# Counting edges per block: sums of two one-hot columns instead of four, and more matmuls to add them

## The chip, the cores and the metric

The kernel runs on one core of a Trainium2 chip. A core has five engines that run their own instruction streams: TensorE (PE in the profile, its weight loads PEld), VectorE (DVE), ScalarE (ACT), GpSimd (POOL) and SyncE (SP, which here only issues DMAs). They wait for one another by semaphores. The metric is the device time of one execution in microseconds (us); lower is better. Times are compared as medians of several runs.

## The reference

A graph with 3125 nodes (256 features each) and 103125 edges `src`, `dst`, `edge_weight1`. Cut to what matters:

```
h   = layernorm(x)
msg = silu(concat(h[src], h[dst], edge_weight) @ mW1 + mb1)
msg = silu(layer_norm(msg) @ mW2 + mb2)
agg = segment_sum(msg, src, 3125)
x   = x + h + silu(concat(h, agg) @ uW1 + ub1) @ uW2 + ub2
# then a feed-forward layer for the 1561 nodes with the highest router score
```

`setup_inputs` sorts the edges by `dst`, so `src`, by which messages are summed, comes in no order. The kernel has to sort the edges by the block of `src` first.

## The kernel before

The 3125 nodes are cut into 25 blocks of 125. The program has these stages, one after the other: counting and placing (up to about 160 us), routing of edge records into sorted order (to about 410 us), the edge stage with the two message layers (to about 1800 us) and the node stage. The change touches the first alone.

**What counting computes.** Each of 128 partitions holds 806 edges. They are handled in 62 supersteps of 13 columns (`COLS`), two supersteps to a *group*, so there are 31 groups (`i` in the code). For every edge the stage finds its place among the edges of the same block: how many edges of that block stand before it. In a group:

- `equal(i)` (VectorE, L700) writes the one-hot tile `eq`: for each of the 2 x 13 columns of edges, 25 numbers that are 1 where the edge's block is b. That is 650 elements in a partition. `eq` is a ring of four groups (`EQR`), and `equal` is called three groups ahead.
- `sums(i)` (GpSimd, L490 and L495) adds neighbouring columns: `two[t] = eq[t] + eq[t-1]`, then `four[t] = two[t] + two[t-2]`, with zero columns in front. `two` is one buffer, `four` a ring of two.
- `totals(i)` (TensorE, L578) adds up whole supersteps: four matmuls with a matrix of ones over columns 0, 4, 8 and 12 of `four`, 50 elements wide (both supersteps at once).
- ScalarE (L343) copies this total out of PSUM into `tot`. Between two such copies it has other work: casts of the edge data and the sums and squares of layernorm (`tallies`).
- `count(i)` (TensorE, L587 and L589) makes, in a PSUM bank for each superstep, the number of equal blocks before each edge. One matmul with a strictly triangular matrix counts within a column (325 wide), and matmuls with ones add the earlier columns of the superstep: with sums of four columns these are shifted by 1, 5 and 9 columns and 300, 200 and 100 elements wide.
- `starts(i)` (VectorE, L708, L710, L712) makes from `tot` where each block begins, and `bases(i)` (TensorE, L597, two matmuls 325 wide) adds it to the same banks.
- `select(i)` (VectorE, L720 and L725) multiplies the banks with `eq` and reduces over the 25 blocks; that is the edge's place.

**The order of the work** is written out by hand. TensorE in step i: `totals(i+1)`, `count(i)`, `bases(i-1)`. VectorE in step i: `starts(i)`, `select(i-1)`, `equal(i+3)`. GpSimd: `sums(i)` and behind it, in six of the groups, one piece of other work over all 806 columns (`plane`). Every engine runs its instructions in this order, so an instruction that waits holds up all behind it. GpSimd's `four(i)` waits until `count(i-2)` has read the ring's buffer (`s_cnt`), and `count(i)` waits for `select(i-3)` (`s_sel`), for three pairs of banks.

After the last `select` VectorE goes on by itself with the places of all edges, and routing follows.

Of the kernel before, what the change touches and what calls it, by code (L numbers as in the profile page):

```python
# [6 lines left out]
BF16 = mybir.dt.bfloat16  # L7
# [3 lines left out]
ALU = mybir.AluOpType  # L11
# [3 lines left out]
P = 128  # L15
# [3 lines left out]
BLOCKS = NODES // NB  # L19
COLS = 13  # L20
# [12 lines left out]
ROWS = TILES * P + P * WIN + P  # L33
DG = PAIRS // RING
EQR = 4
PCOLS = 3
PRING = 4
LAST = 18
# [12 lines left out]
def build(nc, io):  # L51
# [17 lines left out]
    with ExitStack() as whole:  # L69
        def alloc(stack, name, shape, dt):  # L70
            return stack.enter_context(nc.sbuf_tensor(name, shape, dt))

        def semaphore(stack, name):
            return stack.enter_context(nc.semaphore(name))
# [35 lines left out]
        with ExitStack() as ctx:  # L110
            def sb(name, shape, dt):
                return alloc(ctx, name, shape, dt)

            def sem(name):
                return semaphore(ctx, name)
# [12 lines left out]
            vals = sb("vals", [P, EC, PLANES], BF16)  # L128
            eq_words = EQR * 2 * (COLS + 1) * BLOCKS // 2
            eq = x_all[:, 6 * EC:6 * EC + eq_words].bitcast(BF16).rearrange("p (r h t b) -> p r h t b", r=EQR, h=2, b=BLOCKS)  # L130
            two = sb("two", [P, 2, COLS + 2, BLOCKS], BF16)
            four = sb("four", [P, 2, 2, COLS, BLOCKS], BF16)
            prod = sb("prod_e", [P, 2 * COLS, BLOCKS], F32)
            place = x_all[:, 2 * EC:3 * EC]
            r_all = x_all[:, 3 * EC:4 * EC]
# [19 lines left out]
            tb_i = sb("tb_i", [P, PG], I32)  # L155
            or_ = sb("or_", [P, 2, COLS - PCOLS, P], BF16)
            orp = [half[:, k * PCOLS * P // 2:(k + 1) * PCOLS * P // 2].bitcast(BF16).rearrange("p (t r) -> p t r", t=PCOLS)
                   for half in (f1, f2) for k in range(PRING // 2)]
# [3 lines left out]
            onesb = sb("onesb", [P, P], BF16)  # L162
# [60 lines left out]
            s_f1 = sem("s_f1")  # L223
            s_eq = sem("s_eq")
            s_sums = sem("s_sums")
            s_four = sem("s_four")
            s_base = sem("s_base")
            s_cnt = sem("s_cnt")
            s_fresh = sem("s_fresh")
# [189 lines left out]
            def _(pool):  # L419
# [1 line left out]
                pool.memset(dst_i[:, TAIL:EC], 0).then_inc(s_pads, 1)  # L421
                pool.memset(ew_f[:, TAIL:EC], 0.0).then_inc(s_pads, 1)
                pool.memset(eq[:, :, :, 0:1, :], 0.0).then_inc(s_sums, 1)
                pool.memset(two[:, :, 0:2, :], 0.0).then_inc(s_sums, 1)
                pool.memset(mb1_z[:, :], 0.0).then_inc(s_mb1, 1)
                pool.memset(onesb[:, :], 1.0).then_inc(s_pool, 1)
                pool.iota(iota_n[:, :], pattern=[[1, P]], base=0, channel_multiplier=0,
# [55 lines left out]

                def sums(i):
                    pool.wait_ge(s_eq, i + 1)
                    if i:
                        pool.wait_ge(s_four, i)
                    else:
                        pool.wait_ge(s_sums, 2)
                    pool.tensor_tensor(two[:, :, 2:COLS + 2, :], eq[:, i % EQR, :, 1:COLS + 1, :],  # L490
                                       eq[:, i % EQR, :, 0:COLS, :], ALU.add).then_inc(s_sums, 1)
                    pool.wait_ge(s_sums, i + 3)
                    if i >= 2:
                        pool.wait_ge(s_cnt, i - 1)
                    pool.tensor_tensor(four[:, i % 2, :, :, :], two[:, :, 2:COLS + 2, :], two[:, :, 0:COLS, :],  # L495
                                       ALU.add).then_inc(s_four, 1)

                def last_row():
                    pool.wait_ge(s_last, 16)
                    pool.wait_ge(s_to_all, 1)  # L500
                    pool.wait_ge(s_pool, 19)
                    pool.wait_ge(s_four, 4)
                    pool.tensor_copy(w_parts[WP:P, 0, :], w_last[WP:P, :]).then_inc(s_parts, 1)
                    pool.wait_ge(s_parts, 1)
                    pool.tensor_tensor(w_parts[WP:P, 1, :], w_last[WP:P, :], w_parts[WP:P, 0, :],
                                       ALU.subtract).then_inc(s_parts, 1)
                    pool.wait_ge(s_parts, 2)

                for i in range(SUPERS // 2):
                    sums(i)  # L510
                    if i == 3:
                        last_row()
                    plane(i)
                    if i == 16:
                        pool.wait_ge(s_tally, BLOCKS)
                        pool.tensor_scalar(neg_mean[:, :], tally[:, 0, :], -1.0 / D, None, ALU.mult).then_inc(s_mean, 1)
# [10 lines left out]
                def pool_columns(s):  # L527
                    if s >= PRING:
                        pool.wait_ge(s_win, s - PRING + 1)
                    for k in range(PCOLS):  # L530
                        c = s * COLS + COLS - PCOLS + k
                        ins = pool.tensor_scalar(orp[s % PRING][:, k, :], iota_n[:, :], r_all[:, c:c + 1], None,
# [34 lines left out]
            def _(pe):  # L567
                pe.wait_ge(s_pool, 3)

                def bank(s):  # L570
                    return psK[:, 2 * (s // 2 % 3) + s % 2, 0:COLS * BLOCKS].rearrange("p (t b) -> p t b", b=BLOCKS)

                def totals(i):
                    pe.wait_ge(s_four, i + 1)
                    if i:
                        pe.wait_ge(s_tot, i)
                    for t in range(0, COLS, 4):
                        mm = pe.matmul(psX[:, 0:2 * BLOCKS].rearrange("p (h b) -> p h b", h=2), onesb[:, :],  # L578
                                       four[:, i % 2, :, t, :], start=(t == 0), stop=(t == COLS - 1))
                    mm.then_inc(s_totp, 1)  # L580

                def count(i):
                    if i >= 3:
                        pe.wait_ge(s_sel, i - 2)
                    for h in range(2):
                        to = bank(2 * i + h)
                        pe.matmul(to[:, :, :], tri[:, :], eq[:, i % EQR, h, 1:COLS + 1, :], start=True, stop=False)  # L587
                        for d in range(1, COLS, 4):
                            mm = pe.matmul(to[:, d:COLS, :], onesb[:, :], four[:, i % 2, h, 0:COLS - d, :],  # L589
                                           start=False, stop=False)  # L590
                    mm.then_inc(s_cnt, 1)

                def bases(i):
# [6 lines left out]
                    mm.then_inc(s_rank, 1)  # L600

                totals(0)
                for i in range(SUPERS // 2 + 1):
                    if i < SUPERS // 2:
                        if i + 1 < SUPERS // 2:
                            totals(i + 1)
                        count(i)
                    if i:
                        bases(i - 1)
# [4 lines left out]
                for k in range(2):  # L614
                    mm = pe.matmul(psC[0:1, 0:D], bcol[:, k:k + 1], w2raw[:, k, :], start=(k == 0), stop=(k == 1))
# [24 lines left out]
                def route(s):  # L640
# [4 lines left out]
                    for t in range(COLS):  # L645
                        marks = or_[:, s % 2, t, :] if t < COLS - PCOLS else orp[s % PRING][:, t - COLS + PCOLS, :]
                        mm = pe.matmul(psK[:, s % 3, 0:PLANES * WIN], marks,
# [18 lines left out]
                for g in range(TG):  # L666
# [4 lines left out]
                    for k, plane in enumerate((0, 4, 5)):  # L671
                        mm = pe.transpose(psR[:, g % 2, k, 0:n], recT[0:n, g, :, plane], identb[0:n, 0:n])
# [3 lines left out]
            def _(dve):  # L676
# [21 lines left out]
                def equal(i):  # L698
                    c = 2 * COLS
                    V.tensor_tensor(eq[:, i % EQR, :, 1:COLS + 1, :],  # L700
                                    blk[:, i * c:(i + 1) * c].rearrange("p (h t) -> p h t", h=2).unsqueeze(3).broadcast_to(
# [67 lines left out]
                def windows(s):  # L769
                    if s >= 2:  # L770
                        dve.wait_ge(s_win, s - 1)
                    own = slice(s * COLS, (s + 1) * COLS)
                    mine = slice(s * COLS, (s + 1) * COLS - PCOLS)
                    V.tensor_tensor(or_[:, s % 2, :, :],
# [785 lines left out]
```

## Time and profile before

| | us |
|---|---|
| median of 3 runs | 2132.21 (2132.2 to 2133.16) |
| the profiled execution | 2126.56 |
| its span, first to last instruction | 2124.8 |
| counting: first `equal` to the end of the last `select` | 15.8 to 154.0 |
| PE busy, whole span | 1848.7 (87%) |
| DVE busy, whole span | 1847.5 (87%) |
| POOL busy, whole span | 1483.0 (70%) |

A row of the timeline has the start in us from the span's start, the length in us, the engine, the line, the operation, what it writes and reads, and the shape; `x3` means three instructions merged; in brackets stands how long the engine was idle before it and what ended that. A group's row has the number of instructions, the busy time, the mean of one in ns, and the idle time before them. Matmuls overlap: a matmul's own length (from its start until its result has left the array) is longer than the distance to the start of the next one. Matmul rows with `x2` or more span from the first start to the last end.

### The profile page before, as it was taken

To read this page: it belongs to the slowest core of one execution; us is meant where nothing else is said; L and a number is where in the kernel's file an instruction comes from. 1 tells how busy PE (TensorE), PEld (TensorE's weight loads), DVE (VectorE), ACT (ScalarE), POOL (GpSimd) and SP (SyncE) were. 2 spreads that over 40 slices of the span, in tenths; PEclk is the share of its full clock that TensorE was granted. 3 is DMA by queue.
4 is the path that set the end of the run, shared out by engine and by line. 5 is a ranking of instruction groups with operands and counts; after the bars stand their busy time and mean duration, and the time that the engine had idled before them with its cause. 6 is when DMAs were issued, how large, how long until landed. Compare 5 with 4: busy or idle time off the path is not lost. (4 is left out here: it accounts for less than half of the span.)

```text
span 2124.8 us, 46537 instructions
## 1 busy us (share of the span) xinstructions
PE 1848.7 (87%) x11277; PEld 1603.5 (75%) x11278; DVE 1847.5 (87%) x4642; ACT 1501.9 (71%) x3084; POOL 1483.0 (70%) x1393
## 2 busy tenths in 40 slices
PE   3554665259999999999999999999999999799996
PEld 1333554258999999999999989999999899577775
DVE  5788999568999999999999999999999999655895
ACT  2322332149999999999999999999999999323322
POOL 8767888487888888888888888888888886503000
PEclk9996887579999999999999999999999999899998
DMA  4000000245333333333333333433333335101001
GB/s 133 1 0 12 30 30 25 90 121 160 104 104 101 107 100 107 103 103 104 104 104 101 106 101 107 102 105 104 104 104 101 106 102 65 43 1 21 10 1 61
DMA packets 109820, 169.16 MB, mean 80 GB/s; under 512 B 42785, under 2 KB 79571, under 8 KB 109517
## 3 DMA queue, kind: packets, MB, share of 16 engines
q0 software_dynamic: 43168, 114.55, 21.1%
q1 hardware_dynamic: 61086, 48.90, 7.5%
q10 hardware_dynamic: 5516, 5.08, 0.8%
q8 instruction: 26, 0.43, 0.1%
q14 instruction: 24, 0.20, 0.0%
HBM read 156.30 MB, written 11.74 MB: 79 GB/s over the span
## 5 line engine op out<-in xcount | busy, mean ns | idle before, releaser
L961 POOL DMA_INDIRECT g_rows<-b_table,idx_ring x816 | 849.4, 1041 | 237.2 <-issue 212.3
L1097 PE MATMUL ps<-w2g,nT 128*128 128x256 f32 x3432 | 815.4, 381 | 1.2 <-ACT rec L997 1.2
L1097 PEld LDWEIGHTS ps<-w2g,nT 128*128 128x128 f32 x3432 | 620.8, 191 | 68.6 <-ACT rec L997 1.4
L1004 ACT ACTIVATE normed<-act,rec 128x255 f32<-128x255 f32 x858 | 467.6, 596 | 88.0 <-DVE rec L1162 83.5
L1069 PE MATMUL psH<-a_sb,ohT 128*128 x1716 | 345.3, 324 | 43.2 <-DVE ohT L1176 39.4
L1069 PEld LDWEIGHTS psH<-a_sb,ohT 128*128 128x128 f32 x1716 | 257.9, 192 | 97.7 <-issue 74.9
L1196 DVE BATCH_NORM_STATS2 rec<-act 128x6 f32<-128x256 f32 x858 | 316.6, 409 | 1.9 <-ACT act L1018 1.9
L1202 DVE TENSOR_TENSOR low<-rec,high 128x512 fp32r<-128x512 f32 x429 | 301.5, 703 | 1.1 <-ACT high L1010 1.1
L1190 DVE TENSOR_TENSOR g_rows<-psH,g_rows 128x512 f32<-128x512 f32 x429 | 292.5, 682 | 10.0 <-DMA g_rows<-b_table,rec 8.3
L1018 ACT ACTIVATE act<-g_rows 128x512 f32<-128x512 f32 x429 | 267.5, 624 | 19.7 <-DVE g_rows L1190 19.5
L1010 ACT ACTIVATE high<-rec 128x512 fp32r<-128x512 f32 x429 | 266.7, 622 | 0.2
L997 ACT ACTIVATE rec<-ps 128x512 f32<-128x512 f32 x429 | 251.3, 586 | 11.8 <-PE psG L1080 11.8
L1089 PE MATMUL psM<-identf,normed 128*128 128x128 f32 x1716 | 258.7, 273 | 0.5 <-ACT nT L1014 0.5
L1014 ACT ACTIVATE nT<-psM 128x512 f32<-128x512 f32 x429 | 249.4, 581 | 3.9 <-PE ps L1097 3.9
L950 POOL TENSOR_TENSOR rec<-rec,exph 128x6 f32<-128x6 f32 x143 | 224.2, 1568 | 15.2 <-DVE rec L1154 12.2
L1079 PE MATMUL psG<-high,ohf 128*125 128x256 f32 x858 | 223.3, 283 | 11.7 <-DVE agg L1129 11.7
L1080 PE MATMUL psG<-low,ohf 128*125 128x256 f32 x858 | 223.5, 282 | 0.0
L1089 PEld LDWEIGHTS psM<-identf,normed 128*128 128x128 f32 x1716 | 201.0, 141 | 0.7 <-issue 0.7
L1181 DVE TENSOR_TENSOR ohf<-rec 128x250 fp32r<-128x250 f32 x429 | 185.9, 433 | 0.0
L1129 DVE TENSOR_TENSOR agg<-psG,agg 125x256 f32 x429 | 176.3, 411 | 0.6 <-PE psG L1080 0.4
L1079 PEld LDWEIGHTS psG<-high,ohf 128*125 128x125 f32 x858 | 159.4, 186 | 14.8 <-DVE low L1202 14.4
L1176 DVE TENSOR_SCALAR ohT<-loc_rows,node_col 125x256 fp32r<-125x256 bf16 x429 | 163.1, 380 | 4.3 <-DMA loc_rows<-loc_d 4.3
(206 smaller groups left out, 2397.3 us busy)
## 6 DMA issues: line engine op xcount, KB each, us to landing
loc_rows<-loc_d SPq DMA_DIRECT2D x143, 187.5 KB
g_rows<-b_table,idx_ring POOLq DMA_INDIRECT x816
h_sb<-in_x SPq DMA_DIRECT2D x1, 3125.0 KB
b_table<-b_out SPq DMA_DIRECT2D x25, 125.0 KB
x_all<-in_x ACTq DMA_DIRECT2D x1, 3125.0 KB
out<-x_all SPq DMA_DIRECT2D x5, 625.0 KB
ohT<-ew_d SPq DMA_DIRECT2D x143, 9.0 KB
idx_ring<-rec SPq DMA_DIRECT2D x136, 3.0 KB
```

Of the source, the lines that this page charges most:

```text
L961: pool.indirect_dma_start(g_rows[:, j, n, :], None, b_table[:, :], bass.IndirectOffsetOnAxis(ap=which, axis=0)).then_inc(s_gather[j], 16)
L997: nc.scalar.activation(msg[:, (j - 15) % 3, :, :], ps2[:, (j - 15) % 2, :, :], ACT.Silu).then_inc(s_msg, 1)
L1004: ins = nc.scalar.activation(normed[:, (j - 10) % 2, n, 0:D - 1], act1[:, (j - 10) % RING, n, 0:D - 1], ACT.Identity, scale=rstd_e[:, g % ...
L1010: nc.scalar.activation(high[:, (j - 15) % 3, :, :], msg[:, (j - 15) % 3, :, :], ACT.Copy).then_inc(s_high, 1)
L1018: nc.scalar.activation(act1[:, (j - 4) % RING, :, :], g_rows[:, (j - 4) % RING, :, :], ACT.Silu).then_inc(s_act1, 1)
L1069: mm = pe.matmul(psH[:, j % 2, n, :], ohT[:, k, n, :], rows, start=(part == 0), stop=(part == 1))
L1079: pe.matmul(to, ohf[:, k, n, :], high[:, k, n, :], start=(n == 0), stop=False)
L1089: mm = pe.transpose(psM[:, (j - 11) % 2, n, q, :], normed[:, (j - 11) % 2, n, q * P:(q + 1) * P], identf[:, :])
L1097: mm = pe.matmul(ps2[:, (j - 13) % 2, n, :], nT[:, (j - 13) % 2, n, q, :], w2g[:, q, :], start=(q == 0), stop=(q == 1))
L1190: V.tensor_tensor(g_rows[:, k, :, :], psH[:, j % 2, :, :], g_rows[:, k, :, :], ALU.add).then_inc(s_hid, 1)
L1196: ins = V.bn_stats(stat[:, q // 3, 2 * (q % 3) + n, :, :].rearrange("p h w -> p (h w)"), act1[:, q, n, :])
L1202: V.tensor_tensor(low[:, k, :, :], msg[:, k, :, :], high[:, k, :, :], ALU.subtract).then_inc(s_low, 1)
```

## The change

GpSimd no longer makes `four`. `sums(i)` is one instruction, which writes `two` in a ring of three groups, without the zero columns in front. `count` therefore needs matmuls with ones at shifts 1, 3, 5, 7, 9 and 11 (300, 250, 200, 150, 100 and 50 wide) for each superstep, and `totals` seven matmuls, over columns 0, 2, ..., 12. The wait of GpSimd for TensorE is now for `count(i-3)`.

```diff
+TWOS = 3
-            two = sb("two", [P, 2, COLS + 2, BLOCKS], BF16)
-            four = sb("four", [P, 2, 2, COLS, BLOCKS], BF16)
+            two = sb("two", [P, TWOS, 2, COLS, BLOCKS], BF16)
...
-                pool.memset(two[:, :, 0:2, :], 0.0).then_inc(s_sums, 1)
...
                 def sums(i):
                     pool.wait_ge(s_eq, i + 1)
-                    if i:
-                        pool.wait_ge(s_four, i)
-                    else:
-                        pool.wait_ge(s_sums, 2)
-                    pool.tensor_tensor(two[:, :, 2:COLS + 2, :], eq[:, i % EQR, :, 1:COLS + 1, :],
-                                       eq[:, i % EQR, :, 0:COLS, :], ALU.add).then_inc(s_sums, 1)
-                    pool.wait_ge(s_sums, i + 3)
-                    if i >= 2:
-                        pool.wait_ge(s_cnt, i - 1)
-                    pool.tensor_tensor(four[:, i % 2, :, :, :], two[:, :, 2:COLS + 2, :], two[:, :, 0:COLS, :],
-                                       ALU.add).then_inc(s_four, 1)
+                    if i == 0:
+                        pool.wait_ge(s_sums, 1)
+                    if i >= TWOS:
+                        pool.wait_ge(s_cnt, i - TWOS + 1)
+                    pool.tensor_tensor(two[:, i % TWOS, :, :, :], eq[:, i % EQR, :, 1:COLS + 1, :],
+                                       eq[:, i % EQR, :, 0:COLS, :], ALU.add).then_inc(s_two, 1)
...
-                    pool.wait_ge(s_four, 4)
+                    pool.wait_ge(s_two, 4)
...
                 def totals(i):
-                    pe.wait_ge(s_four, i + 1)
+                    pe.wait_ge(s_two, i + 1)
...
-                    for t in range(0, COLS, 4):
+                    for t in range(0, COLS, 2):
                         mm = pe.matmul(psX[:, 0:2 * BLOCKS].rearrange("p (h b) -> p h b", h=2), onesb[:, :],
-                                       four[:, i % 2, :, t, :], start=(t == 0), stop=(t == COLS - 1))
+                                       two[:, i % TWOS, :, t, :], start=(t == 0), stop=(t == COLS - 1))
...
-                        for d in range(1, COLS, 4):
-                            mm = pe.matmul(to[:, d:COLS, :], onesb[:, :], four[:, i % 2, h, 0:COLS - d, :],
+                        for d in range(1, COLS, 2):
+                            mm = pe.matmul(to[:, d:COLS, :], onesb[:, :], two[:, i % TWOS, h, 0:COLS - d, :],
                                            start=False, stop=False)
```

TensorE's order in one step of counting, before: the second superstep's `count` (325, 300, 200 and 100 wide; `tri` is the triangular matrix, `onesb` the ones, `x_all` holds `eq`), then `bases`, then the next `totals`.

```order
L587 MATMUL psK<-x_all,tri 128x325
L589 MATMUL psK<-four,onesb 128x300
L589 MATMUL psK<-four,onesb 128x200
L589 MATMUL psK<-four,onesb 128x100
L597 MATMUL psK<-we,onesb 128x325 x2
L578 MATMUL psX<-four,onesb 128x50 x4
```

The same place on TensorE with the change:

```order
L581 MATMUL psK<-x_all,tri 128x325
L583 MATMUL psK<-two,onesb 128x300
L583 MATMUL psK<-two,onesb 128x250
L583 MATMUL psK<-two,onesb 128x200
L583 MATMUL psK<-two,onesb 128x150
L583 MATMUL psK<-two,onesb 128x100
L583 MATMUL psK<-two,onesb 128x50
L591 MATMUL psK<-we,onesb 128x325 x2
L572 MATMUL psX<-two,onesb 128x50 x7
```

The order of the calls is the same; each superstep's `count` has three matmuls more and each `totals` three more.

GpSimd's order around group 4, before (`a_sb` is written by the `plane` pieces):

```order
L467 TENSOR_TENSOR a_sb<-a_sb,vals 128x806
L490 TENSOR_TENSOR two<-x_all 128x2x325
L495 TENSOR_TENSOR four<-two 128x650
L490 TENSOR_TENSOR two<-x_all 128x2x325
L495 TENSOR_TENSOR four<-two 128x650
L470 TENSOR_SCALAR a_sb<-a_sb 128x806
```

The same place and a little further on with the change:

```order
L466 TENSOR_TENSOR a_sb<-a_sb,vals 128x806
L489 TENSOR_TENSOR two<-x_all 128x650 x2
L469 TENSOR_SCALAR a_sb<-a_sb 128x806
L489 TENSOR_TENSOR two<-x_all 128x650 x2
L472 TENSOR_SCALAR a_sb<-a_sb 128x806
```

Each group has one instruction on GpSimd where it had two; the pieces of other work keep their places. VectorE's and ScalarE's orders are unchanged.

## Rows read from the trace of the kernel before

**Rows 1.** The page: TensorE's granted clock in 40 slices, in tenths.

```profile
PEclk9996887579999999999999999999999999899998
```

**Rows 2.** Waits in 40 to 150 us: total us, times, longest.

```profile
DVE prod_e L720 <- PE psK L597: 24.8, 19, 2.1
```

**Rows 3.** Timeline, 109.4 to 118.4 us: one circle over two groups.

```profile
109.45 0.83 DVE L700 TENSOR_TENSOR x_all<-x_all,psV 128x650 bf16<-128x650 f32 x1
...
110.36 1.42 POOL L490 TENSOR_TENSOR two<-x_all 128x650 bf16<-128x650 bf16 x1 [0.61 <-DVE x_all L700]
...
111.87 1.30 POOL L495 TENSOR_TENSOR four<-two 128x650 bf16<-128x650 bf16 x1
...
113.22 0.35 PE L578 MATMUL psX<-four,onesb 128*128 128x50 bf16 x4 [0.96 <-POOL four L495]
...
113.39 0.45 PE L587 MATMUL psK<-x_all,tri 128*128 128x325 bf16 x1
...
114.10 0.83 DVE L700 TENSOR_TENSOR x_all<-x_all,psV 128x650 bf16<-128x650 f32 x1
...
114.85 0.24 DVE L708 SCALAR_TENSOR_TENSOR sm<-agg,psV 128x50 f32<-128x50 f32 x1
...
114.92 0.74 PE L597 MATMUL psK<-we,onesb 128*128 128x325 bf16 x2
...
115.78 0.83 DVE L720 TENSOR_TENSOR prod_e<-psK,x_all 128x650 f32<-128x650 f32 x1
...
116.64 0.83 DVE L725 TENSOR_REDUCE x_all<-prod_e 128x26 f32<-128x650 f32 x1
117.51 0.83 DVE L700 TENSOR_TENSOR x_all<-x_all,psV 128x650 bf16<-128x650 f32 x1
```

**Rows 4.** Timeline, 145 to 154 us: the last groups.

```profile
149.22 0.75 PE L597 MATMUL psK<-we,onesb 128*128 128x325 bf16 x2
149.71 0.24 DVE L708 SCALAR_TENSOR_TENSOR sm<-agg,psV 128x50 f32<-128x50 f32 x1
...
150.53 0.83 DVE L720 TENSOR_TENSOR prod_e<-psK,x_all 128x650 f32<-128x650 f32 x1
...
150.56 0.61 PE L597 MATMUL psK<-we,onesb 128*128 128x325 bf16 x2 [0.58 <-DVE we L712]
...
153.14 0.83 DVE L725 TENSOR_REDUCE x_all<-prod_e 128x26 f32<-128x650 f32 x1
```

**Rows 5.** PE alone in four stretches: length, busy (instructions), granted clock, DMA.

```profile
109.80:117.80 8.00, 4.89 (x28) 1.00 0.00 0
145.40:150.90 5.50, 4.89 (x26) 1.00 0.00 0
...
229.40:232.80 3.40, 0.80 (x15) 1.00 0.16 47
178.20:181.60 3.40, 1.69 (x19) 1.00 0.00 2
```

**Rows 6.** Timeline, 36 to 40 us: the wait for the node rows.

```profile
36.08 0.42 ACT L338 ACTIVATE b_out<-h_sb 125x256 f32<-125x256 f32 x1 [8.50 <-DMA h_sb<-in_x]
...
37.28 0.32 PE L578 MATMUL psX<-four,onesb 128*128 128x50 bf16 x4 [5.55 <-ACT agg L343]
...
39.81 0.83 DVE L720 TENSOR_TENSOR prod_e<-psK,x_all 128x650 f32<-128x650 f32 x1 [1.85 <-PE psK L597]
```

**Rows 7.** Groups of GpSimd in 15 to 154 us.

```profile
L521 POOL TENSOR_TENSOR rstd<-rstd,exph 125x25 f32<-125x25 f32 x1 | 4.4, 4362 | 0.1
L482 POOL TENSOR_TENSOR vals<-a_sb 128x806 bf16<-128x806 f32 x1 | 2.9, 2898 | 0.0
L470 POOL TENSOR_SCALAR a_sb<-a_sb 128x806 f32<-128x806 f32 x1 | 2.3, 2282 | 0.0
```

**Rows 8.** Groups in 109.8 to 117.8 us: weight loads of `count` and of `totals`.

```profile
L589 PEld LDWEIGHTS psK<-four,onesb 128*128 128x128 bf16 x12 | 1.7, 145 | 0.9
...
L578 PEld LDWEIGHTS psX<-four,onesb 128*128 128x128 bf16 x8 | 0.4, 115 | 4.4 <-POOL four L495 4.4
```

More of the change, by code:

```diff
@@ L225, in build @@
             s_sums = sem("s_sums")
-            s_four = sem("s_four")
+            s_two = sem("s_two")
             s_base = sem("s_base")
```

## The prediction

> **What bounds the kernel now.** I read the page first, for the clock and the stages, then the timeline of counting, since the change touches nothing else, and last the waits there. In counting no engine is busy throughout. The waits name a circle: VectorE waits for the matmuls of `bases`, 24.8 us in all [rows 2], GpSimd waits for VectorE's `equal` (0.61 us, rows 3), and TensorE waits for GpSimd's `four` [rows 3]. The timeline gives its length [rows 3]. From an `equal` at 109.45: 0.91 us to the start of `two`, 1.51 from there to `four`, 1.35 to `totals`, 0.17 to `count`, 1.53 to `bases`, 0.86 to `select` and 1.73 to the `equal` two groups on, at 117.51. That is 8.06 us for two groups (two such circles run interleaved), or 4.03 a group. Over groups 2 to 27 the mean is somewhat longer, 4.19 us: the pieces of other work on GpSimd, 2.3 to 2.9 us each [rows 7], delay the circle now and then.
>
> The start is held by something else. ScalarE waits 8.50 us for the DMA of the node rows, and with it TensorE for the copy of a total, until 37.28 [rows 6]. What the change gains before that is lost there; only from 37.28 on does it count.
>
> At the end VectorE's last `select` ends at 153.97 [rows 4] and the stages behind it start from there, so a shorter counting moves all that follows, one to one.
>
> **The clock in counting.** The page's clock digits show nearly full speed in the first slices [rows 1], and the windows 1.00 [rows 5], but the matmuls tell otherwise. Of two matmuls of 325 columns at 149.22, the whole takes 0.75 us; at 150.56, after the engine had worked from 145.4 almost without a pause (4.89 of 5.50 us, rows 5), the same pair takes 0.61. The 0.14 saved is 325 columns at 1.2 GHz less 325 at 2.4 (0.27 − 0.135). And `count` before takes 1.53 us for 1850 columns, 0.83 ns a column, which is 1.2 GHz. So I take counting as running at 1.2 GHz up to 150 us. The Trainium skill ("TensorE: Matmul & The Clock Gate", Part 1) says that half rate is the default and that activity releases it, and gives start-to-start distances of N/1.2 and N/2.4 ns plus 2.5; by it the row's 1.00 can't be a granted full clock. The spacing here agrees with the skill, the window's figure doesn't.
>
> **The change part by part.**
>
> *GpSimd.* `four` goes: 1.35 us of the circle. `two` stays at 1.42, plus the 0.05 that `four` shows between its end and `totals` (1.35 − 1.30), so 1.47. Its output is now contiguous; I expect no difference, since `four` with the same 650 elements took 1.30, which bounds a gain at 0.12 us a circle. The removed memset lies before the first `equal` and costs nothing. The new ring wait is for `count(i-3)`. It never holds: `two(i)` waits for `equal(i)`, which stands behind `select(i-2)` and so behind `count(i-1)`. Queued behind it would be the pieces of other work, which nobody waits for closely.
>
> *TensorE.* `totals`: seven matmuls where four took 0.17, so 0.30. `count`: 2 x (325 + 300 + 250 + 200 + 150 + 100 + 50) = 2750 columns, at 1.2 GHz 2.29 us; at 2.4 GHz 1.15, and I take 1.20 for small gaps. `bases` is unchanged, 0.54 us of issue at 1.2 GHz and 0.27 at 2.4, by which its 0.86 to `select` falls to about 0.59.
>
> *The circle after, at 1.2 GHz:* 0.91 + 1.47 + 0.30 + 2.29 + 0.86 + 1.73 = 7.56, or 3.78 a group against 4.03. *At 2.4 GHz:* 0.91 + 1.47 + 0.30 + 1.20 + 0.59 + 1.73 = 6.20, or 3.10.
>
> *VectorE is late next.* Its own work of a group is 0.82 from L708 to L720 [rows 4], 0.86, 0.87, and 0.75 from `equal` to the next L708 [rows 3]: 3.30 us. So at 2.4 GHz not the circle but VectorE sets 3.30 a group. At 1.2 GHz the circle sets 3.78, and TensorE's own work is 0.30 + 2.29 + 0.54 = 3.13 a group.
>
> *Which clock?* Before, TensorE worked 4.89 us of 8.00 in counting and stayed at 1.2 GHz. With the change it works 3.13 of 3.78 a group, and from 37.28 on `totals`, `count`, `bases`, `totals`, `count`, `bases` follow without a pause for 6.2 us, since two groups of `two` are ready by then. The clock had risen by 150.56 after 4.89 of 5.50 us [rows 4, 5]. So I expect the rise in the 40s. Does it stay up? At 2.4 GHz TensorE works some 0.30 + 1.20 + 0.27 = 1.77 us of 3.30, and about 0.2 more with the tails. In 178.2 to 181.6 it worked 1.69 of 3.40 and the clock was at 1.00; before a fall (229.4 to 232.8) it had worked 0.80 of 3.40 [rows 5]. The new load lies nearer the first, so I take it to stay up.
>
> *The sum.* From `totals` at 37.28: `count` ends at 39.87, `select(2)` starts at 40.73, which is 0.92 later than before [rows 6], as `count` is longer and still slow. `select(3)` 3.30 later, 44.03. `equal(6)` at 42.46 leads by 0.91 + 1.47 + 0.30 + 2.29 + 0.86 to `select(4)` at 48.29. From there VectorE sets the pace: `select(5)` 51.6, `select(27)` 22 x 3.30 later, 124.2. The last three have no `equal`: 2.55, 2.55 and 1.73, and 1.73 for the last itself: 132.8, and 0.3 for the circle in the tail, 133.1. Against 153.97 that is 20.9. I take off 1 us for the 2.9 us piece on GpSimd (it makes `two` 1.1 us late; the circle has 0.4 to spare for two groups) and similar, and 1 us for a clock that rises a group later: 18.9, say 19. GpSimd's 4.36 us power for layernorm [rows 7] stays covered: it starts when the last `two` is done, some 2.4 us after the last `equal`, ends at 7.1, and VectorE needs it 10.2 after that `equal`.
>
> The profiled execution at 2126.56 would become 2107.6. The median of the runs is 2132.21, 5.7 above that execution with the same program; I take 19 from it: **2113**.
>
> **The rivals.**
>
> 1. *The clock stays at 1.2 GHz in counting.* For: it did so in all steady groups before, and in rows the rise needs near-continuous work. Against: 3.13 of 3.78 us and the 6.2 us run. The same sum: `select(4)` at 48.3, 23 groups at 3.78 to `select(27)` at 135.2, then 3.7, 3.1, 1.73 and 1.73 for the tail: 145.5. Gain 8.5, less 0.5 for GpSimd: **2124**.
>
> 2. *The clock goes up and down.* At 2.4 GHz the engine pauses half of each group; if that lets it fall, the next groups run at 3.78, work is dense again, and it rises again. Routing shows such a change to and fro, at 0.80 us of work in 3.40 before a fall. Half the groups at each pace: 25 x 0.24 = 6 less than my sum, gain 13: **2119**. The Trainium skill (the same page, "A second HAM failure mode") describes matmul groups with small idles between them in which the clock oscillates; this is that rule, and no row of counting shows it yet, as the clock never rose there before 150.
>
> 3. *Slower: the weight loads of short matmuls show.* Each matmul has its own load, 145 ns in `count` and 115 in `totals` [rows 8]. If a matmul can't start sooner than 0.15 after the one before, `totals` takes 1.05 and `count` 2 x (0.27 + 0.25 + 0.21 + 4 x 0.15) = 2.66, together 3.71. The piece that they replace is 1.35 + 0.17 + 1.53 = 3.05, and from `two` 0.05 stays, so the change loses where both take over 3.00 us (it is 2.59 by columns). The circle becomes 8.7, 4.35 a group, 25 groups at +0.32 and the start: about +9, **2141**. Against it: the four 50-column matmuls of `totals` start within 0.17 us now, 42 ns apart, with 115 ns loads. The skill's page says, in Part 3, that weight loads overlap with running matmuls only for other row groups; by that this rival would be the forecast, but the 42 ns speak against it.
>
> 4. *Nothing to measure:* a gain under 4 us, where the rest gives it back: routing or the edge stage starting at a bad moment of TensorE's clock costs a few us at most. It needs rival 1 and this together: about **2130**.
>
> **How the numbers follow.** My case 0.62 (its own range 2110 to 2117, from 21 gained with nothing lost to 15 with a few slow groups), rival 2 0.16, rival 1 0.12, rival 4 0.06, rival 3 0.04. A difference under 0.2%, 4.3 us, can't be told from none here. Faster is then 0.90, same 0.06, slower 0.04. The range takes in my case, rivals 2 and 1: 2109 to 2126.
>
> **What would show it.** In the profile after: matmul pairs of `bases` of 0.75 us only up to the 40s, 0.61 or less behind that; `select` to `select` 3.30 us from about 50 on; VectorE's wait for `bases`, 24.8 us before, at a few us; `totals` in 0.47 us with seven matmuls; the last `select` ending at 134 to 135. Pairs of 0.75 throughout and 3.78 a group would be rival 1, a mixture rival 2, `totals` starts 0.1 or more apart rival 3. I am wrong altogether if counting ends before 140 and the whole is not shorter by as much.

## The result, and the profile after

| | before | after |
|---|---|---|
| median | 2132.2 us (4 runs) | 2108.86 us (4 runs, 2106.06 to 2111.7) |
| ratio | | 0.9896, 95% interval 0.9884 to 0.9908 |
| profiled execution, span | 2126.56, 2124.8 | 2107.55, 2105.8 |
| end of the last `select` | 154.0 | 132.5 |

23.3 us less, 1.1%; forecast were 19, to 2113. The measured median lies 0.14 us below the stated range, which began at 2109: the sign and the mechanism were right, and the size was somewhat too cautious.

The timeline after, one circle over two groups, answers to [rows 3]. The lines have moved: L694 is `equal`, L489 `two`, L572 `totals`, L581 and L583 `count`, L591 `bases`, L714 and L719 `select`, L702 the start of `starts`.

```profile
99.07 0.83 DVE L694 TENSOR_TENSOR x_all<-x_all,psV 128x650 bf16<-128x650 f32 x1
...
99.98 1.42 POOL L489 TENSOR_TENSOR two<-x_all 128x650 bf16<-128x650 bf16 x1 [1.88 <-DVE x_all L694]
...
101.46 0.35 PE L572 MATMUL psX<-two,onesb 128*128 128x50 bf16 x7 [1.46 <-POOL two L489]
...
101.65 0.30 PE L581 MATMUL psK<-x_all,tri 128*128 128x325 bf16 x1
...
102.85 0.45 PE L591 MATMUL psK<-we,onesb 128*128 128x325 bf16 x2
...
103.93 0.83 DVE L714 TENSOR_TENSOR prod_e<-psK,x_all 128x650 f32<-128x650 f32 x1
...
104.80 0.83 DVE L719 TENSOR_REDUCE x_all<-prod_e 128x26 f32<-128x650 f32 x1
...
105.67 0.83 DVE L694 TENSOR_TENSOR x_all<-x_all,psV 128x650 bf16<-128x650 f32 x1
```

Two groups take 6.60 us, 3.30 each, where they took 8.06. `count`, 2750 columns, lasts 1.20 us from L581 to L591: 0.44 ns a column, the 2.4 GHz rate; the pair of `bases` takes 0.45 us against 0.74 in [rows 3]. `select` starts 1.08 us after `bases` though some 0.6 would do, and its row has no idle time in brackets: VectorE was busy with what stands before it.

The waits in 40 to 133 us (total, times, longest) answer to [rows 2]:

```profile
POOL two L489 <- DVE x_all L694: 46.2, 21, 10.1
...
PE psX L572 <- POOL two L489: 36.8, 25, 2.1
DVE prod_e L714 <- PE psK L591: 3.2, 3, 2.7
```

VectorE's wait for `bases` fell from 24.8 us to 3.2, and 2.7 of that is the one after the DMA stall. The others now wait for VectorE.

TensorE in two stretches between changes of its clock (length, busy and instructions, granted clock, busy share of the DMA engines, GB/s), which answer to [rows 5]:

```profile
37.30:42.70 5.40, 4.96 (x39) 0.50 0.58 231
42.80:131.40 88.60, 48.72 (x601) 1.00 0.00 1
```

Behind the dense work right after the stall, 4.96 of 5.40 us, the clock rose at 42.8, and it stayed up to the end of counting, with TensorE busy 48.72 of 88.60 us. Here the matmul spacing and the granted clock agree. Before, the granted clock read 1.00 while the spacing was that of 1.2 GHz; that profile has no record of the clock before 150.9.

The start, which answers to [rows 6]:

```profile
37.63 0.25 DVE L702 SCALAR_TENSOR_TENSOR sm<-agg,psV 128x50 f32<-128x50 f32 x1 [7.70 <-ACT agg L343]
37.74 0.45 PE L572 MATMUL psX<-two,onesb 128*128 128x50 bf16 x7 [11.11 <-ACT agg L343]
...
41.16 0.83 DVE L714 TENSOR_TENSOR prod_e<-psK,x_all 128x650 f32<-128x650 f32 x1 [2.74 <-PE psK L591]
```

TensorE waits 11.11 us where it waited 5.55: the groups before were done sooner, and all of that went into the wait behind the DMA of the node rows.

### The profile page after: what moved, and what is told of

Its sections match the earlier page's. It is cut to its first block and busy times, and to the rows that moved or that the text cites. A ratio compares the mean times of both kernels' runs of the same rounds, so it can differ in the third digit from the quotient of the medians.

```text
span 2105.8 us, 47032 instructions
## 1 busy us (share of the span) xinstructions
PE 1828.9 (87%) x11556; PEld 1600.4 (76%) x11557; DVE 1849.6 (88%) x4642; ACT 1502.1 (71%) x3084; POOL 1443.2 (69%) x1361
```

## The experiments

Every kernel's profile gives the start of `select(27)`, the mean group from `select(4)` to it, and the time from the start of the last `select` to the end of the span, which the change doesn't touch:

| | select(27) | us a group | rest of the span | median |
|---|---|---|---|---|
| before | 144.5 | 4.17 | 1972.5 | 2132.2 |
| before again | 144.8 | 4.17 | 1980.2 | (2134.6, one run) |
| after | 123.7 | 3.30 | 1975.1 | 2108.9 |
| after again | 124.9 | 3.37 | 1974.3 | 2108.2 |
| before, TensorE filled | 138.2 | 3.89 | 1973.9 | 2123.9 |
| after, second addition kept | 147.6 | 4.30 | 1978.2 | 2134.8 |
| the same, TensorE filled | 145.3 | 4.23 | 1974.3 | 2129.5 |
| after, ring of two | 125.5 | 3.38 | 1975.7 | 2111.0 |
| after, roundings on ScalarE | 120.2 | 3.19 | 1976.4 | 2108.0 |
| the same, last piece moved | 117.6 | 3.08 | 1977.8 | 2104.3 |

The rows ran on different chips; runs of the kernel before beside them had medians of 2131.95 and 2130.18. Judge counting by the profiles and the whole by the ratios below, which are always to the kernel before on the same chip.

**Is the clock part of it? The kernel before, with TensorE filled.**

```diff
+FILL = 8
...
                     if i:
                         bases(i - 1)
+                    if i + 1 < SUPERS // 2:
+                        if i >= 2:
+                            pe.wait_ge(s_sel, i - 1)
+                        for _ in range(FILL):
+                            pe.matmul(psK[:, 2 * ((i + 1) % 3), 0:P], onesb[:, :], tri[:, :], start=True, stop=True)
```

> The kernel before, with four column sums, and eight extra matmuls of 128 columns in every group behind bases, in TensorE's pauses (their result is overwritten by the next count). Theory (part of the gain is TensorE's clock, which rises to 2.4 GHz when the engine works more of each group): bases pairs of 0.61 us instead of 0.75 from the first dense groups on, the circle 8.06 less 0.76 of count and 0.27 of bases, 7.03 us for two groups, 3.5 a group instead of 4.03 to 4.19; some 13 us less, about 2119. Rival (the clock is not what counts, GpSimd's shorter sums are all of it): 4.2 a group as before, 2132, or slower by what the extra matmuls delay.

Measured: 2123.92 us, ratio 0.9966 (0.9954 to 0.9979). More work, done sooner. The clock rose, but did not stay: 3.89 us a group on average. TensorE in three stretches with different clocks, and two matmuls of `bases` and the extra ones in the last undisturbed groups:

```profile
50.00:66.00 16.00, 6.95 (x84) 1.00 0.01 2
67.00:70.00 3.00, 2.89 (x22) 0.50 0.00 0
70.50:73.50 3.00, 1.15 (x15) 1.00 0.00 0
```

```profile
127.55 0.83 DVE L726 TENSOR_TENSOR prod_e<-psK,x_all 128x650 f32<-128x650 f32 x1
...
130.62 0.45 PE L598 MATMUL psK<-we,onesb 128*128 128x325 bf16 x2
130.92 0.61 PE L615 MATMUL psK<-tri,onesb 128*128 128x128 bf16 x8
...
134.52 0.83 DVE L726 TENSOR_TENSOR prod_e<-psK,x_all 128x650 f32<-128x650 f32 x1
```

From one `select` to the next but one, 127.55 to 134.52, are 6.97 us (7.03 expected), and so it is in eight circles in a row from 110 us on, where the clock stayed at 2.4 GHz. Where it fell in between, circles took 8.0 to 9.6; the longest of them also hold a piece of GpSimd's other work, as the 9.6 and 10.0 of the kernel before do. So the clock alone shortens the old circle by 1.1 us of 8.06.

**Does GpSimd's part count? The changed kernel with a second addition.**

```diff
                     pool.tensor_tensor(two[:, i % TWOS, :, :, :], eq[:, i % EQR, :, 1:COLS + 1, :],
-                                       eq[:, i % EQR, :, 0:COLS, :], ALU.add).then_inc(s_two, 1)
+                                       eq[:, i % EQR, :, 0:COLS, :], ALU.add).then_inc(s_add, 1)
+                    pool.wait_ge(s_add, i + 1)
+                    pool.tensor_tensor(spare[:, :, :, :], two[:, i % TWOS, :, :, :], two[:, i % TWOS, :, :, :],
+                                       ALU.add).then_inc(s_two, 1)
```

> The changed kernel, and GpSimd makes a second sum of the same size into a spare tile before it tells TensorE, so that GpSimd's part of the circle is as before (1.51 + 1.35 us) while TensorE's matmuls are the new ones. Theory with the clock up and staying up: circle 0.91 + 1.51 + 1.35 + 0.30 + 1.20 + 0.59 + 1.73 = 7.59, 3.80 a group against 3.30; about 12 us above the changed kernel, 2121, and still below the kernel before. With the clock low: 8.95, 4.48 a group, 2138, above the kernel before. A rival by which GpSimd is not on the path gives 2109.

Measured: 2134.75 us, ratio 1.0014 (1.0003 to 1.0026). The whole gain is gone, and a little more. GpSimd's addition took 1270 ns each, the circle 7.98 us with the clock mostly up and 8.9 to 9.1 otherwise, against 7.59 and 8.95 expected. The clock did not stay, so neither of the two expected times came, but one between, 4.30 us a group. It alternated like this:

```profile
57.50:64.10 6.60, 2.86 (x40) 1.00 0.01 2
64.30:71.00 6.70, 4.30 (x31) 0.50 0.00 0
71.20:77.80 6.60, 2.76 (x40) 1.00 0.00 0
78.00:88.00 10.00, 7.75 (x54) 0.50 0.01 2
```

TensorE was busy 2.86 and 2.76 of 6.60 us before the falls; in the changed kernel it was busy 48.72 of 88.60, and the clock held. The busy time does not decide alone: in the first experiment the clock held from 50 to 66 us with 6.95 busy of 16.00.

**Would more fill hold it up?** `FILL = 6` added to the kernel above, with the same edit as in the first experiment.

> The kernel with GpSimd's second addition kept and TensorE's new matmuls, and six extra matmuls of 128 columns a group in TensorE's pauses. Without them the clock went up and down and the mean group took 4.30 us, the two-group circle 7.98 at best and 8.9 while the clock was low. Theory (the falls of the clock cost the difference): with more work in each group the clock stays up, 3.99 us a group, the last groups 8 us sooner, about 2127, below the kernel before. Rival (the additions themselves on GpSimd make it slow): 4.3 us a group or more, 2135 or above.

Measured: 2129.54 us, ratio 1.0001 (0.9988 to 1.0013). The theory half failed: the clock still fell six times between 43 and 150 us. Most circles with the clock up took 7.41 us, less than the 7.98 that I had taken for the floor, and the mean group 4.23. Circles with a fall took up to 10.9 us against 7.41, though the longest also hold a piece of GpSimd's other work; that this much more work prevents the falls does not hold. A likely reason, not tested in this kernel, is that the extra matmuls don't fill a pause in which TensorE waits for GpSimd behind one of its long pieces.

**Is VectorE the bound? Two of its operations moved to ScalarE.**

```diff
+                    nc.scalar.activation(sm[:, 0, :, 1:BLOCKS + 1], psX[:, 0:2 * BLOCKS].rearrange("p (s b) -> p s b", s=2),
+                                         ACT.Copy, bias=WIN / 2 - 0.75).then_inc(s_st, 1)
                     nc.scalar.activation(tot[:, :, 2 * i:2 * i + 2].rearrange("p b s -> p s b"),
...
+                    nc.scalar.activation(sm[:, 0, :, 1:BLOCKS + 1], sm[:, 0, :, 1:BLOCKS + 1],
+                                         ACT.Copy, bias=MAGIC_W).then_inc(s_st, 1)
...
+                    nc.scalar.activation(sm[:, 1 + i % 2, :, 1:BLOCKS + 1], sm[:, 0, :, 1:BLOCKS + 1],
+                                         ACT.Copy, scale=1.0 / P, bias=-MAGIC_W / P).then_inc(s_st, 1)
...
-                    link(V.scalar_tensor_tensor(out=sm[:, 0, :, 1:BLOCKS + 1], in0=tot[:, :, 2 * i:2 * i + 2].rearrange("p b s -> p s b"),
-                                                scalar=WIN / 2 - 0.75, in1=magic_v.rearrange("p (s b) -> p s b", s=2), op0=ALU.add, op1=ALU.add))
-                    link(V.scalar_tensor_tensor(out=sm[:, 1, :, 1:BLOCKS + 1], in0=sm[:, 0, :, 1:BLOCKS + 1], scalar=-MAGIC_W,
-                                                in1=part_v.rearrange("p (s b) -> p s b", s=2), op0=ALU.add, op1=ALU.mult))
```

> The changed kernel with the two small VectorE operations of starts (0.51 us of VectorE a group) made on ScalarE, in three operations. Theory (VectorE's own work sets 3.30 us a group, the circle would allow 3.10): VectorE's work falls to 2.79, the circle sets 3.10; 25 groups at 0.20, about 5 us less, 2104. Rival (something else than VectorE sets 3.30): no difference. If ScalarE with three more operations a group comes too late: slower.

Measured: 2107.98 us, ratio 0.9896 (0.9876 to 0.9916). In counting the theory holds: most circles take 6.06 us, 3.03 a group, and VectorE waits for TensorE again (total, times, longest, 44 to 128 us):

```profile
DVE prod_e L725 <- PE psK L606: 11.4, 15, 2.7
```

So 3.30 was VectorE's own work, and the circle allows 3.03, not the 3.10 that was forecast. `select(27)` starts 3.5 us sooner, not 5: two circles took 8.7 and 8.2 us, when the clock fell at 86.5. In the median the 3.5 us do not show.

**What makes the clock fall there?** The last of GpSimd's long pieces, 2.9 us, runs just before. It was moved behind counting, first with the roundings on ScalarE, then alone in the changed kernel.

```diff
-                    plane(i)
+                    if i != 18:
+                        plane(i)
...
                 pool.tensor_tensor(rstd[:, :], rstd[:, :], exph[0:NB, :], ALU.pow).then_inc(s_rstd1, 1)
+                plane(18)
```

> The kernel with the roundings of starts on ScalarE, and the last piece of GpSimd's other work (2.9 us, group 18) moved behind the layernorm power, after counting. In the run before, this piece made TensorE's clock fall once and the two groups around it take 8.7 instead of 6.06 us. Theory: 3.03 us a group throughout, the last select 2.4 us sooner than there and some 6 us sooner than in the changed kernel; about 2103. Rival (the fall of the clock has another cause, or the piece then holds up routing): as before the move, about 2105 to 2108.

Measured: 2104.31 us, the median of three runs, ratio 0.9876 (0.9856 to 0.9895), the fastest version; these three, 2103.15 to 2104.41, lie below all four of the changed kernel on the same chip (2106.21 to 2109.99). A fourth run took 3836 us and is in neither figure. The clock stays up from 40.6 to 125.9 us, and all circles from group 14 up to the last groups take 6.06 or 6.07. Before group 14 some take up to 6.89, as they did without the move, so the mean is 3.08 a group and not 3.03.

> The changed kernel, unchanged, on the same chip as the others, to set the improved version beside it: 2109 within 3 us, 3.30 us a group.

Measured: 2108.18 us. This second profile of the changed kernel had a fall of the clock that the first had not. In its timeline GpSimd's piece is L481:

```profile
84.36 2.91 POOL L481 TENSOR_TENSOR vals<-a_sb 128x806 bf16<-128x806 f32 x1
...
86.99 1.42 POOL L489 TENSOR_TENSOR two<-x_all 128x650 bf16<-128x650 bf16 x1
...
88.46 0.47 PE L572 MATMUL psX<-two,onesb 128*128 128x50 bf16 x7 [2.16 <-POOL two L489]
...
89.00 1.09 PE L583 MATMUL psK<-two,onesb 128*128 128x300 bf16 x6
...
91.89 0.83 DVE L714 TENSOR_TENSOR prod_e<-psK,x_all 128x650 f32<-128x650 f32 x1 [1.70 <-PE psK L591]
```

`two` is late by 0.7 us, TensorE pauses 2.16 instead of 1.46, the clock falls at 88.3, six matmuls take 1.09 us and not 0.62, and VectorE waits 1.70: two interleaved circles of 8.25 for 6.59, by which all behind comes 1.66 us later. TensorE had been busy 1.84 us in the 4.2 before:

```profile
84.00:88.20 4.20, 1.84 (x23) 1.00 0.00 0
88.40:91.60 3.20, 3.14 (x24) 0.50 0.00 0
```

The first profile of the changed kernel has the same place 0.36 us later. There TensorE paused as long and had done as much, and the clock did not fall; the piece cost 0.15 us in each of the two circles:

```profile
88.80 0.35 PE L572 MATMUL psX<-two,onesb 128*128 128x50 bf16 x7 [2.14 <-POOL two L489]
```

```profile
84.36:88.56 4.20, 1.84 (x23) 1.00 0.00 0
```

So the pause and the work before it do not settle whether the clock falls. What does stays open.

> The changed kernel with only the last piece of GpSimd's other work (2.9 us, group 18) moved behind the layernorm power. Two of three profiles of the changed kernel (one of them with a ring of two) show one fall of TensorE's clock at 88 to 89 us, just behind this piece, and two circles of 8.2 us for 6.59. Theory (the piece makes the sum of group 19 late, TensorE pauses, and the clock may fall, by where in time the pause lies): no fall between 43 and 131 us, 3.30 us a group throughout, about 1 us below the changed kernel on average, 2107 to 2108. Rival (the falls come by chance wherever): a fall here too.

Measured: no fall; the clock stays at 2.4 GHz and all circles take 6.59 to 6.60 us up to the last groups.

```profile
42.30:130.80 88.50, 48.77 (x602) 1.00 0.01 1
```

Measured were 2251.64 us, but the times can't be set beside the others: on this chip the kernel before took 2262.68 us (ratio of this kernel 0.9949, 0.9923 to 0.9975). In the two profiles from this chip the edge stage is 134 and 141 us longer, and counting is not. The gain over the kernel before is 11.0 us here, half of the 22.0 on the chip of the repeat, though counting was as short; why is open, since the kernel before has no profile from this chip. Three profiles with the piece moved (two of them from this chip, with the next experiment's) show no fall there, against three of four with the piece in place that do. That speaks for the piece as what gives the occasion; the first profile of the changed kernel shows that the fall doesn't always come. Whether the move alone saves time in the whole was not shown, as the changed kernel was not run on this chip.

> The improved version once more, unchanged. One of its four executions took 3836 us, the three others 2103.2 to 2104.4. Theory (a disturbance of the chip that has nothing to do with the kernel): all near 2104, and about 4 us below the changed kernel. Rival (the edit has a rare slow case): another execution far above.

Measured: 2249.12 us on that slow chip, ratio 0.9942 (0.9922 to 0.9962), 12 runs from 2242.5 to 2255.3. No run far above came again; what made the one of 3836 us stays open. The 4 us below the changed kernel could not be tested here either; the runs overlap with those of the experiment before. Counting was as in the first run but for one other fall of the clock at 45 us, 3.07 us a group.

**Does the third buffer matter?** `TWOS = 2`.

> The changed kernel with a ring of two for the sums instead of three, so that GpSimd waits for count(i-2). Theory (that wait never ends last, since equal(i) stands behind count(i-1)): no difference, 2109. Rival (the third buffer carries part of the gain by letting GpSimd run ahead): slower by some us, groups above 3.30 us.

Measured: 2110.98 us, ratio 0.991 (0.9894 to 0.9927). I had said that the wait never ends last; with two buffers it does, eight times (44 to 133 us):

```profile
POOL two L489 <- DVE x_all L694: 22.2, 12, 1.9
POOL two L489 <- PE psK L583: 15.3, 8, 2.9
```

The reasoning was off by two groups: VectorE's order puts `equal(i)` behind `select(i-4)`, not `select(i-2)`, and so behind `count(i-3)` only. That covers the wait of a ring of three, for `count(i-3)`, and not that of a ring of two. The ring of two costs little: five circles of 6.71 to 6.87 us instead of 6.59, `select(27)` 0.6 us later than in the repeat of the changed kernel, which had a fall of the clock too. The 2.8 us between the medians are more than counting explains; the rest of the span was 1.4 us longer in this profile.

**How much does one profile say?**

> The kernel before, unchanged, for a second profile: the first profiled execution took 2126.56 us and the runs without a profile 2132.2. If profiled executions differ among themselves by the phase in which TensorE's clock changes come, this one may lie elsewhere between 2126 and 2133, with the difference in routing or the start of the edge stage; if a profile always takes less, it is near 2126.6 again.

Measured: 2134.56 us. Counting is the same to 0.3 us; after it, the rest took 1980.2 us and not 1972.5. Over all profiles on undisturbed chips this rest lies between 1972.5 and 1980.2, with no relation to the change (table). So the first profile of the kernel before had a short rest by chance. What sets the rest from run to run was not looked into.

## Why the prediction was right, point by point

- *The circle.* Right. Its terms hold: `two` to `totals` 1.48 (forecast 1.47), `count` 1.20 (1.20), `select` to `equal` 1.74 (1.73). One was too large: seven matmuls of `totals` before `count` take 0.19 us (101.46 to 101.65) and not 0.30. At 2.4 GHz they start 25 ns apart, except that the second starts 39 ns behind the first. `bases` to `select` was a little too large as well, 0.56 for 0.59 in the kernel with the roundings on ScalarE. That makes 6.06 of the 6.20, 3.03 a group and not 3.10.
- *The clock in counting before was 1.2 GHz.* Right, shown by the filled kernel: the same `bases` pair in 0.45 us, a circle 1.1 us shorter with more work in it. One reading behind it was wrong: the pair of 0.61 us at 150.56 lies across the rise of the clock at 150.9, and a pair wholly at 2.4 GHz takes 0.45, 0.30 less than at 1.2.
- *The clock rises after the stall and stays up.* Right for the first profile, from 42.8 to 131.5. In the repeat it fell once, which cost 1.66 us. The 1 us that I took off for a clock that rises a group later did not come. Rival 2, the clock up and down, came true in the variants with a longer circle, and in this kernel only as that one fall.
- *VectorE is late next, 3.30.* Right to the hundredth, and confirmed by taking work off VectorE.
- *What happens before the stall is lost.* Right: 11.11 us of wait for 5.55.
- *The ring wait never holds.* True from 40 to 133 us; before the stall it held once, for 1.6 us, which the stall took up. The step behind it was wrong: in steady groups `equal(i)` stands behind `count(i-3)`, not `count(i-1)` (the ring of two, above).
- *The start and the end.* `select(2)` at 41.16 (40.73), as `totals` began 0.46 later; `select(3)` 44.45 (44.03). From there it went better than I had it: `select(4)` at 47.75, not 48.29, because the clock had risen before `count(5)`. The last `select` started at 130.76 and ended at 132.5; my sum said 133.1, before I took off 2 us for the piece on GpSimd and a late clock. Of these 2 us, 0.15 came: the piece made `two` 0.7 us late and not 1.1.
- *The total.* 2107.6 for the profiled execution, measured 2107.55, is luck: counting gave 21.5 us, 2.6 more than my 18.9, and the rest took 2.6 more than in the first profile. The median, 2113 against 2108.86, shows the mis-sized terms: the 2 us taken off, and 0.6 of the sum. What is left of the 23.3, some 2 us, is in the spread of the rest.
- *Rival 3, weight loads of short matmuls.* It did not occur: 25 ns between matmuls whose loads take about 0.1 us each. The Trainium skill's sentence ("TensorE: Matmul & The Clock Gate", Part 3) that loads overlap only with matmuls on other rows of the array is not what these traces show, where loads on all 128 rows run beside the matmuls before them. Its Part 1 gives a floor of about 25 ns between starts, and there the trace agrees.
- *Rivals 1 and 4, the clock stays low, and nothing to measure:* did not occur. The give-back in the rest that rival 4 prices at a few us had no row behind it; the rest varied by 7.7 us over the profiles on undisturbed chips, with no relation to the change.

How the gain divides can be told only roughly, since the two parts depend on one another. The clock alone (four-column sums, clock up) makes a circle of 6.97 from 8.06. Shorter sums with the clock up make 6.06, and VectorE holds that at 6.60. With the longer sums on GpSimd back and the new matmuls kept, nothing is gained. The remaining corner, shorter sums at 1.2 GHz throughout, was not measured; by the sum it is 7.56.

## What to carry to other kernels

When engines take turns in a circle, none of them busy throughout, add the lengths of the steps around it, and then each engine's own work: the larger sets the pace, and here it passed from the circle to VectorE. Moving work from GpSimd onto TensorE cost less here than it seemed, because the clock rose from 1.2 to 2.4 GHz with it: `count` took 1.53 us for 1850 columns before and 1.20 for 2750 after. Check the clock by the distance between matmuls, not by the profile's figure alone. Look also at what pauses the engine afterwards: behind a single 2.9 us piece on GpSimd the clock fell in three profiles of four, and in the repeat of the changed kernel that cost 1.7 us.

## What the runs showed that was not expected

- Extra matmuls with no use made the old kernel 0.34% faster (2123.92 against 2131.95 us).
- In the changed kernel the clock held at 2.4 GHz while TensorE worked 48.72 of 88.60 us; in the variant with the second addition it fell time and again, after 2.86 and 2.76 us of work in 6.60. Two profiles of the changed kernel have the same pause of TensorE, 2.14 and 2.16 us, behind the same 1.84 us of work in 4.20; the clock held in one and fell in the other.
- On one chip the kernel before took 2262.68 us and not 2130 to 2132. In the two profiles from it the edge stage was 134 and 141 us longer, and counting as on the other chips.
